# Cross-attention by quadrants of 32 queries: sums of squares as rows of 256 columns, query sums turned on VectorE, key weights rounded by ScalarE

## The chip, the cores and the metric

The kernel runs on one core of one Trainium2 chip. The metric is the device time of one execution in microseconds. Before the change it is 654.05 us, the median of 3 runs (654.0 to 654.47).

## The reference

1024 tokens of 256 features go through a gated cross-attention to a context of 1024 rows of 128 features (16 sequences of 64 tokens, each with its own 64 context rows, 16 heads of 128), and then through a gated block of causal self-attention and a mixture of experts (16 experts, 6 taken, and a shared one). All weights and tokens are float32. The change touches the cross-attention alone:

```python
x = x + tanh(g_xattn[0]) * xattn(layernorm(x), ctx_1024, Wq, Wk, Wv, Wo, gq, gk)

def xattn(hidden, ctx, Wq, Wk, Wv, Wo, gq, gk):
    q = (hidden @ Wq).reshape(B, Sq, H, D)       # B = 16, Sq = 64, H = 16, D = 128
    k = (ctx @ Wk).reshape(B, Skv, H, D)         # Skv = 64
    v = (ctx @ Wv).reshape(B, Skv, H, D)
    q = q * rsqrt(mean(q * q, -1) + 1e-5) * gq
    k = k * rsqrt(mean(k * k, -1) + 1e-5) * gk
    attn = softmax(einsum("bqhd,bkhd->bhqk", q, k) / sqrt(D))
    return einsum("bhqk,bkhd->bqhd", attn, v).reshape(B, Sq, H * D) @ Wo
```

## The kernel before

**Stages.** The tokens are handled in two halves of 512 (HT), 8 sequences each. Three kinds of stage follow each other, each for both halves: cross-attention (a), self-attention (b) and the experts' chunks (m). Stage a goes over 8 pairs of heads for each half, so over 16 pairs, and `cross_pair` holds the order of one pair, written out by hand once for each engine. Engines meet by semaphores; a pair `u` is worked on while the projections of the next one (`nxt`) run, the output of the one before (`prev`) is added, and the weights of the one after next (`after`) are split.

**Precision.** Projections and outputs are made in three matmuls of float32r with both operands split in a rounded part (`_hi`) and its rest (`_lo`). The rounded part of the query and key weights is cast by VectorE (`split_queries`, `split_keys`, L1356 and L1368) and the rest is taken by GpSimd (L1573). SyncE loads the next weights into `raw_a` once the rests are taken. Scores, sums of squares and context values are plain float32 matmuls.

**A pair on TensorE** (`cross_pair`): `norm_q` (L659), `scores` (L682), `context_values` of prev (L703), key and query projections of nxt (L525), the two outputs of prev (L552) around the second query projection, in the first half also `value_out` (L648), the turn of the attention (L690), and `norm_k` for nxt (L668). `norm_q` sums the squared queries over the 128 features: the squares of a sequence (64 columns) are the weights and a column of ones streams, so that a sum comes out as one element for each query's partition, 16 matmuls a pair, two column groups of 64. `norm_k` streams the squared keys past 64 columns of ones, 2 matmuls of 512 columns, so that each sum lies in all 64 partitions of its sequence. `scores` makes 64x64 blocks, two sequences above each other.

**The chain beside it.** VectorE adds the variance term of the tokens to the query sums (`add_variance`, L1302), ScalarE takes logarithm and root of both sums (`log_k`, `root_k`, `log_q`, `root_q`; L992, L1001, L988, L997), VectorE multiplies the scores by both roots (`scale_scores`, L1314 and L1317), takes the maximum (L1323), then the rests of prev's context values (`split_context_values`, `pv_lo`, L1290), and subtracts the maximum (L1328). ScalarE takes the exponential, VectorE normalises (L1338) and moves the next queries out of PSUM (`take_q`, L1344), with `split_queries` and `split_keys` in between. ScalarE squares queries and keys (L965, L974) and moves turned rows (`take_rows`, L1011) and context values (`take_context_values`, L1022). TensorE waits for ln_q before it projects into the same bank again, for pv_lo before it adds prev's output, for the attention before its turn, for the squares and qt before `norm_q` and `scores`.

**Pieces of token preparation** are laid beside some pairs by `plan_of` and run on VectorE and ScalarE: in the first half statistics (after pair 3, so ahead of the sums of pair 4), the norm (after pair 4) and the turn (pair 5); in the second half statistics (after pair 8 + 1), norm (after 8 + 2), mean squares on ScalarE (in 8 + 3), scale (after 8 + 4) and turn (8 + 5).

Of the kernel before, what the change touches and what calls it, by code (L numbers as in the profile page):

```python
# [32 lines left out]
P = 128  # L33
# [160 lines left out]
def flamingo_layer(nc, x, ctx_t, ctx, head_a, head_b, pair_v, chunk_m, small, out, shared_units):  # L194
# [15 lines left out]
    GROUPS = 2  # L210
    G = 2 * NT
# [18 lines left out]
    with ExitStack() as stack:  # L230
# [60 lines left out]

        gs, gu = ln_k[:].rearrange("p g k -> p (g k)"), r_k[:].rearrange("p g k -> p (g k)")
# [8 lines left out]
        eps_var, ssq = sb("eps_var", [P, HALVES, NT]), sb("ssq", [P, G])  # L301
# [42 lines left out]
        var_ready, rough = sem("var_ready"), sem("rough")  # L344
# [13 lines left out]
        def sequence_at(u, t, s):  # L358

            if u.kind == "a":  # L360
                return t * SPB + s
            return t // 2 * 4 + s * 2 + t % 2

# [4 lines left out]
        def by_row(ap, row):  # L368

            return ap.rearrange("p h (b r n) -> p h b r n", r=SPB, n=P)[:, :, :, row, :]  # L370
# [146 lines left out]
        def _(pe):  # L517
# [134 lines left out]
            def norm_q(u):  # L652

                pe.wait_ge(A["sq_q"], u.of(1))
                pe.wait_ge(A["qt"], u.of(0))
                for h in range(2):
                    for b in range(NS):
                        t, s = divmod(b, SPB)
                        last = nc.tensor.matmul(bank_q[s * SEQ:(s + 1) * SEQ, h * NT + t:h * NT + t + 1],  # L659
                                                sq_q[:, h, b * SEQ:(b + 1) * SEQ], ones[:], start=True, stop=True)  # L660
                last.then_inc(A["ssq_done"], 1)

            def norm_k(u):

                pe.wait_ge(A["sq_k"], u.of(1))
                for s in range(SPB):
                    keys = sq_k[:].rearrange("p h (t s k) -> p (h t) s k", s=SPB, k=SEQ)[:, :, s, :]
                    last = nc.tensor.matmul(bank_p[s * SEQ:(s + 1) * SEQ, :], ones_of[:], keys, start=True, stop=True)  # L668
                last.then_inc(A["ssk_done"], 1)

            def scores(u):
# [3 lines left out]
                pe.wait_ge(stage["kt"], u.of(1))  # L675
                for h in range(2):
                    for b in range(NS):
                        t, s = b // SPB, b % SPB
                        at = sequence_at(u, t, s) * SEQ
# [4 lines left out]
                last.then_inc(stage["scores"], 1)  # L684
# [76 lines left out]
            def release(held):  # L761
                for semaphore, value in held:
                    pe.wait_ge(semaphore, value)

# [129 lines left out]
        def _(act_e):  # L894
# [95 lines left out]
            def log_k(u):  # L990
                act_e.wait_ge(A["ssk_done"], u.n)
                nc.scalar.activation(ln_k[:], groups(bank_p[:]), ACT.Ln, bias=eps5[:, 0:1]).then_inc(A["ln_k"], 1)  # L992
# [6 lines left out]
            def root_k(u):  # L999
                act_e.wait_ge(A["ln_k"], u.n)  # L1000
                nc.scalar.activation(r_k[:], ln_k[:], ACT.Exp, scale=-0.5).then_inc(A["r_k"], 1)  # L1001
# [734 lines left out]
```

## Time and profile before

| | |
|---|---|
| median of 3 runs | 654.05 us |
| profiled execution | 653.9 us |
| its span (first to last instruction) | 651.8 us |
| TensorE matmul busy | 644.9 us, 99% |
| VectorE busy | 457.5 us, 70% |
| ScalarE busy | 318.4 us, 49% |
| GpSimd busy | 251.4 us, 39% |
| stage a, from the first key sums to the last turn | 13 to 204 us of the span |

The times of the engines are sums over the whole span; matmuls overlap each other in the records, so a busy TensorE is not one at its peak. In the views, PE is TensorE, DVE is VectorE, ACT is ScalarE and POOL is GpSimd. A row of the timeline is one instruction, or a run of like ones, with its start, its length and the operands by the program's names. Two records stand for each plain float32 matmul.

### The profile page before, as it was taken

What the parts mean: (1) busy time and instruction counts of PE and PEld (TensorE: products, weight loads), DVE (VectorE), ACT (ScalarE), POOL (GpSimd) and SP (SyncE); (2) the same over time, 40 slices, a digit from 0 to 9 for tenths busy, and PEclk for the clock granted to TensorE, in tenths of its full rate; (3) what the DMA queues carried; (4) which work ended last, traced back from release to release, by engine and by line L of the source; (5) the groups of instructions that cost most, each with busy time, mean ns of one, the idle gap of its engine ahead of it and who ended that gap; (6) DMA issues with size and microseconds to landing.
All of it is one profiled execution on the core that took longest, in us unless ns stands there. A gap on an engine that the chain in (4) does not pass through costs nothing.

```text
span 651.8 us, 16025 instructions
## 1 busy us (share of the span) xinstructions
PE 644.9 (99%) x6176; PEld 566.5 (87%) x6176; DVE 457.5 (70%) x891; ACT 318.4 (49%) x639; POOL 251.4 (39%) x336
## 2 busy tenths in 40 slices
PE   8999999999999999999999999999999999999997
PEld 6888888888888899999899999988888888888886
DVE  5867776787866788676777798666556987555556
ACT  6756656667663334333343433354476444444443
POOL 3221121121132344433343355425544755555553
PEclk9999999999999999999999999999999999999999
DMA  7522112001002222214222222103323233333332
GB/s 229 176 71 77 49 51 74 26 28 48 26 17 64 68 67 65 84 53 127 67 65 66 66 69 82 49 11 112 97 75 96 73 98 95 99 96 86 92 94 91
DMA packets 36013, 50.15 MB, mean 77 GB/s; under 512 B 4080, under 2 KB 23024, under 8 KB 35952
## 3 DMA queue, kind: packets, MB, share of 16 engines
q1 hardware_dynamic: 35376, 48.81, 25.2%
q8 instruction: 44, 0.72, 0.5%
q10 hardware_dynamic: 576, 0.48, 0.2%
q14 instruction: 17, 0.14, 0.1%
HBM read 48.22 MB, written 1.05 MB: 76 GB/s over the span
## 4 chain that ended last, share of the span: by engine, by line
PE 98%; DMA 1%; DVE 1%; SPq 0%; ACT 0%; issue 0%; DVEq 0%; ACTq 0%
PE acc L552 25%; PE bank_k L525 16%; PE bank_q L525 16%; PE bank_v L525 9%; PE bank_v L638 7%; PE bank_s L525 5%; PE bank_s L682 5%; PE bank_p L703 3%; PE bank_p L668 2%; PE bank_q L659 2%; PE bank_t L690 2%; PE bank_p L720 2%; PE bank_k L648 1%; DMA xt<-in_ctx_t 1%; PE bank_t L720 1%; PE bank_p L729 0%
## 5 line engine op out<-in xcount | busy, mean ns | idle before, releaser
L552 PE MATMUL acc<-wo_hi,pv_hi 128*128 128x256 f32 x328 | 93.1, 284 | 1.3 <-DVE pv_lo L1419 1.3
L552 PE MATMUL acc<-wo_lo,pv_hi 128*128 128x256 f32 x328 | 92.9, 283 | 0.0
L552 PE MATMUL acc<-wo_hi,pv_lo 128*128 128x256 f32 x328 | 92.0, 281 | 0.0
L1573 POOL TENSOR_TENSOR wq_lo<-raw_a,wq_hi 128x256 fp32r<-128x256 f32 x32 | 23.3, 731 | 133.6 <-DVE wq_hi L1356 133.6
L552 PEld LDWEIGHTS acc<-wo_hi,pv_hi 128*128 128x128 f32 x328 | 61.5, 188 | 5.2 <-issue 2.1
L552 PEld LDWEIGHTS acc<-wo_lo,pv_hi 128*128 128x128 f32 x328 | 61.6, 188 | 2.3
L1573 POOL TENSOR_TENSOR wq_lo<-raw_m,wq_hi 128x256 fp32r<-128x256 f32 x50 | 39.7, 793 | 61.7 <-DVE wq_hi L1375 60.2
L552 PEld LDWEIGHTS acc<-wo_hi,pv_lo 128*128 128x128 f32 x328 | 62.3, 190 | 0.0
L1419 DVE TENSOR_TENSOR pv_lo<-raw_a,pv_hi 128x512 fp32r<-128x512 f32 (+1 forms) x51 | 37.0, 727 | 32.5 <-ACT pv_hi L1048 32.3
L525 PE MATMUL bank_q<-xt_hi,wq_hi 128*128 128x512 f32 x144 | 59.8, 415 | 0.0
L970 ACT ACTIVATE kt<-bank_k 128x512 f32<-128x512 f32 x63 | 37.8, 600 | 43.4 <-PE bank_k L525 43.3
L1048 ACT ACTIVATE pv_hi<-raw_a 128x512 fp32r<-128x512 f32 (+1 forms) x51 | 31.7, 624 | 55.3 <-DVE raw_a L1414 52.1
L1406 DVE TENSOR_TENSOR r_k<-ln_k,unit_w 128x512 f32<-128x512 f32 x44 | 32.0, 727 | 35.7 <-ACT ln_k L1039 35.7
L525 PE MATMUL bank_q<-xt_hi,wq_lo 128*128 128x512 f32 x144 | 56.6, 393 | 0.0
L525 PE MATMUL bank_q<-xt_lo,wq_hi 128*128 128x512 f32 x144 | 56.4, 392 | 0.0
L1573 POOL TENSOR_TENSOR wk_lo<-raw_m,wk_hi 128x256 fp32r<-128x256 f32 x50 | 39.4, 788 | 33.7 <-ACT wk_hi L1118 33.5
L1573 POOL TENSOR_TENSOR wv_lo<-raw_v,wv_hi 128x512 fp32r<-128x512 f32 x16 | 20.6, 1288 | 72.6 <-DVE wv_hi L1382 72.6
L525 PE MATMUL bank_k<-xt_lo,wk_hi 128*128 128x512 f32 x114 | 44.8, 393 | 0.0
L525 PE MATMUL bank_k<-xt_hi,wk_hi 128*128 128x512 f32 x114 | 44.7, 392 | 0.0
L525 PE MATMUL bank_k<-xt_hi,wk_lo 128*128 128x512 f32 x114 | 44.6, 391 | 0.0
L1573 POOL TENSOR_TENSOR wq_lo<-raw_b,wq_hi 128x256 fp32r<-128x256 f32 x32 | 24.8, 776 | 49.2 <-DVE wq_hi L1359 49.2
L1573 POOL TENSOR_TENSOR wo_lo<-raw_m,wo_hi 128x256 fp32r<-128x256 f32 x50 | 40.2, 805 | 6.8 <-ACT wo_hi L1112 6.8
(216 smaller groups left out, 1908.2 us busy)
## 6 DMA issues: line engine op xcount, KB each, us to landing
raw_m<-in_chunk_m SPq DMA_DIRECT2D x50, 256.0 KB, 2.7
raw_a<-in_head_a SPq DMA_DIRECT2D x48, 192.0 KB, 2.9
raw_b<-in_head_b SPq DMA_DIRECT2D x32, 256.0 KB, 3.1
raw_m<-in_chunk_m SPq DMA_DIRECT2D x50, 128.0 KB, 2.0
raw_v<-in_pair_v SPq DMA_DIRECT2D x16, 256.0 KB, 2.8
raw_b<-in_head_b SPq DMA_DIRECT2D x32, 128.0 KB, 2.1
xs<-in_x SPq DMA_DIRECT2D x6, 128.0 KB, 3.5
out<-xs SPq DMA_DIRECT2D x3, 256.0 KB, 2.4
```

What stands on the lines that cost most here:

```text
L525: last = nc.tensor.matmul(bank[:], w[:, cols], m(k), start=n == 0, stop=n == 3 * chunks - 1)
L552: last = nc.tensor.matmul(acc[t // 2][:, (t % 2) * D:(t % 2 + 1) * D], w[:, tok], m, start=begins and n == 0, stop=True, skip_group_check= ...
L638: last = nc.tensor.matmul(bank_v[:, b * PAIR:(b + 1) * PAIR], m, w[:, cols], start=n == 0, stop=n == 3 * KD - 1)
L659: last = nc.tensor.matmul(bank_q[s * SEQ:(s + 1) * SEQ, h * NT + t:h * NT + t + 1], sq_q[:, h, b * SEQ:(b + 1) * SEQ], ones[:], start=True ...
L682: last = nc.tensor.matmul(bank_s[s * SEQ:(s + 1) * SEQ, g * SEQ:(g + 1) * SEQ], qt[:, h, tok], kt[:, h, tok], start=True, stop=True)
L703: last = nc.tensor.matmul(by_tile(value_bank(r)[:])[:, :, n, :], ctx_sb[rows, at:at + C], rows_t[rows, n], start=True, stop=True)
L720: last = nc.tensor.matmul(value_bank(r)[c * SEQ:(c + 1) * SEQ, cols], values[rows, n, width], turned[rows, cols], start=True, stop=True)
L970: nc.scalar.activation(kt[:, h], bank[:], ACT.Copy).then_inc(stage["kt"], 1)
L1048: nc.scalar.activation(pv_hi[:, u.parity, part], hh[:, part], ACT.Copy).then_inc(M["hh_hi"], 1)
L1406: nc.vector.tensor_tensor(gu, gs, weights, ALU.mult).then_inc(M["weighted"], 1)
L1419: nc.vector.tensor_tensor(pv_lo[:, u.parity, part], hh[:, part], pv_hi[:, u.parity, part], ALU.subtract)\
L1573: nc.gpsimd.tensor_tensor(lo, raw, hi, ALU.subtract).then_inc(signal, 1)
```

## The change

- `norm_q` and `norm_k` become alike: for each of four groups of sequences (`QUADS`), 32 columns of ones are the weights and 256 columns of squares stream, and the result goes to 32 partitions: 4 matmuls each, 256 columns wide, in place of 16 and of 2. A sum now lies in a row, once for each sequence's key or query, and repeated over the group's 32 partitions.
- The query sums are needed by partition. `add_variance` turns them on VectorE (`transpose` of 128x256, 32x32 blocks) into `sums_t` and adds the variance term to every 32nd element. The variance term is brought to the same order by 8 small matmuls against the unit matrix in the first pair of each half (`place_variance`), and copied to `eps_q` by VectorE.
- `scores` makes 32x64 blocks, half a sequence of queries against its 64 keys, in four column groups: 32 matmuls a pair in place of 16.
- `log_k` and `root_k` take 256 columns in place of 512; `scale_scores` broadcasts their result over the two parts of the queries.
- `take_rows`, `by_row`, `take_context_values` and `split_context_values` follow the new order of the sequences, the host lays out the context by it.
- `split_keys` in stage a, but for the first two pairs, goes from VectorE to ScalarE (`round_keys`), one after each of the two `square_q`.

```diff
+    GROUP = 32
+    QUADS = P // GROUP
...
+        half_wide = [a[:].rearrange("p g k -> p (g k)")[:, 0:HT // 2] for a in (ln_k, r_k)]
...
-        eps_var, ssq = sb("eps_var", [P, HALVES, NT]), sb("ssq", [P, G])
+        sums_t = sb("sums_t", [P, HT // 2])
+        eps_var, eps_q, ssq = sb("eps_var", [P, HALVES, NT]), sb("eps_q", [P, G // 2]), sb("ssq", [P, G])
...
-        def sequence_at(u, t, s):
-            if u.kind == "a":
-                return t * SPB + s
+        def sequence_at(t, s):
...
+        def quads(ap):
+            return ap.rearrange("p h (n j q) -> p h n j q", j=QUADS, q=SEQ)
...
         def by_row(ap, row):
...
-            return ap.rearrange("p h (b r n) -> p h b r n", r=SPB, n=P)[:, :, :, row, :]
+            return ap[:, :, row * HT // 2:(row + 1) * HT // 2]
...
             def norm_q(u):
...
                 pe.wait_ge(A["sq_q"], u.of(1))
...
-                for h in range(2):
-                    for b in range(NS):
-                        t, s = divmod(b, SPB)
-                        last = nc.tensor.matmul(bank_q[s * SEQ:(s + 1) * SEQ, h * NT + t:h * NT + t + 1],
-                                                sq_q[:, h, b * SEQ:(b + 1) * SEQ], ones[:], start=True, stop=True)
+                if u.first:
+                    place_variance(u)
+                for j in range(QUADS):
+                    last = nc.tensor.matmul(bank_q[j * GROUP:(j + 1) * GROUP, 0:HT // 2], ones_of[:, 0:GROUP],
+                                            quads(sq_q[:])[:, :, :, j, :], start=True, stop=True)
...
             def norm_k(u):
...
                 pe.wait_ge(A["sq_k"], u.of(1))
-                for s in range(SPB):
-                    keys = sq_k[:].rearrange("p h (t s k) -> p (h t) s k", s=SPB, k=SEQ)[:, :, s, :]
-                    last = nc.tensor.matmul(bank_p[s * SEQ:(s + 1) * SEQ, :], ones_of[:], keys, start=True, stop=True)
+                for j in range(QUADS):
+                    last = nc.tensor.matmul(bank_p[j * GROUP:(j + 1) * GROUP, 0:HT // 2], ones_of[:, 0:GROUP],
+                                            quads(sq_k[:])[:, :, :, j, :], start=True, stop=True)
...
             def scores(u):
...
+                if u.kind == "a":
+                    for g in range(G):
+                        h, part, n = g // 4, g // 2 % 2, g % 2
+                        for j in range(QUADS):
+                            at = (n * QUADS + j) * SEQ
+                            queries = slice(at + part * GROUP, at + (part + 1) * GROUP)
+                            last = nc.tensor.matmul(bank_s[j * GROUP:(j + 1) * GROUP, g * SEQ:(g + 1) * SEQ],
+                                                    qt[:, h, queries], kt[:, h, at:at + SEQ], start=True, stop=True)
+                    last.then_inc(A["scores"], 1)
+                    return
...
-                        at = sequence_at(u, t, s) * SEQ
+                        at = sequence_at(t, s) * SEQ
...
-                last.then_inc(stage["scores"], 1)
+                last.then_inc(B["scores"], 1)
...
+            def place_variance(u):
+                pe.wait_ge(eps_ready, u.half + 1)
+                variance = eps_var[:, u.half, :].rearrange("p (n t) -> p t n", n=2)
+                for j in range(QUADS):
+                    for part in range(2):
+                        row = j % 2 * SEQ + part * GROUP
+                        nc.tensor.matmul(bank_q[j * GROUP:(j + 1) * GROUP, HT // 2 + part * 2:HT // 2 + part * 2 + 2],
+                                         ident[:, row:row + GROUP], variance[:, j // 2], start=True, stop=True)
...
             def log_k(u):
...
-                nc.scalar.activation(ln_k[:], groups(bank_p[:]), ACT.Ln, bias=eps5[:, 0:1]).then_inc(A["ln_k"], 1)
+                nc.scalar.activation(half_wide[0], bank_p[:, 0:HT // 2], ACT.Ln, bias=eps5[:, 0:1]).then_inc(A["ln_k"], 1)
...
             def root_k(u):
...
-                nc.scalar.activation(r_k[:], ln_k[:], ACT.Exp, scale=-0.5).then_inc(A["r_k"], 1)
+                nc.scalar.activation(half_wide[1], half_wide[0], ACT.Exp, scale=-0.5).then_inc(A["r_k"], 1)
...
             def take_rows(u):
...
-                nc.scalar.activation(rows_t[:].rearrange("p n h q -> p h n q"), by_tile(bank_t[:]), ACT.Copy)\
+                nc.scalar.activation(rows_t[:].rearrange("p n h (a q) -> p (h a) n q", q=GROUP),
+                                     bank_t[:].rearrange("p (b n q) -> p b n q", n=QUADS, q=GROUP), ACT.Copy)\
...
             def take_turned(u):
...
-                    nc.scalar.activation(by_row(pv_hi[:], r), value_bank(r)[:].rearrange("p (h b n) -> p h b n", h=2, n=P),
+                    nc.scalar.activation(by_row(pv_hi[:], r), value_bank(r)[:].rearrange("p (h n) -> p h n", h=2),
...
+            def round_keys(u, h, user):
+                act_e.wait_ge(A["k_done"], user.of(h))
+                act_e.wait_ge(ld_a1[h], 16 * u.n)
+                nc.scalar.activation(wk_hi[h][:, 0:P], raw_a1[h][:, AK:AK + P], ACT.Copy).then_inc(A["wk_hi"], 1)
...
             def cross_pair(u):
...
+                after = nxt.next()
...
+                    if after.kind == "a":
+                        round_keys(after, 0, nxt)
...
+                    if after.kind == "a":
+                        round_keys(after, 1, nxt)
...
                     if kind == "x":
-                        link(nc.vector.tensor_scalar(eps_var[:, half, :], mv[:, :, 1], 1e-5, 1e-5, ALU.add, ALU.mult))
+                        nc.vector.tensor_scalar(eps_var[:, half, :], mv[:, :, 1], 1e-5, 1e-5, ALU.add, ALU.mult)\
+                            .then_inc(eps_ready, 1)
...
             def split_context_values(u):
...
-                    nc.vector.tensor_tensor(by_row(pv_lo[:], r), value_bank(r)[:].rearrange("p (h b n) -> p h b n", h=2, n=P),
+                    nc.vector.tensor_tensor(by_row(pv_lo[:], r), value_bank(r)[:].rearrange("p (h n) -> p h n", h=2),
...
             def add_variance(u):
...
-                found = bank_q[:, 0:G].rearrange("p (h t) -> p h t", h=2)
-                nc.vector.tensor_tensor(ssq[:].rearrange("p (h t) -> p h t", h=2), found,
-                                        eps_var[:, u.half, :].unsqueeze(1).to_broadcast([P, 2, NT]), ALU.add)\
+                if u.first:
+                    dve.mark(nc.vector.tensor_copy(eps_q[:], bank_q[:, HT // 2:HT // 2 + G // 2]))
+                link(nc.vector.transpose(sums_t[:], bank_q[:, 0:HT // 2]))
+                found = sums_t[:].rearrange("p (h n a q) -> p h a n q", h=2, n=2, q=GROUP)[:, :, :, :, 0]
+                variance = eps_q[:].rearrange("p (a n) -> p a n", a=2).unsqueeze(1).to_broadcast([P, 2, 2, 2])
+                nc.vector.tensor_tensor(ssq[:].rearrange("p (h a n) -> p h a n", h=2, a=2), found, variance, ALU.add)\
...
             def scale_scores(u):
...
-                    nc.vector.tensor_tensor(sc_sub[:], found, r_k[:], ALU.mult).then_inc(A["raw"], 1)
+                    by_key = half_wide[1].rearrange("p (h n) -> p h n", h=2).unsqueeze(2).to_broadcast([P, 2, 2, P])
+                    nc.vector.tensor_tensor(sc_sub[:].rearrange("p (h a n) k -> p h a (n k)", h=2, a=2),
+                                            bank_s[:].rearrange("p (h a n) -> p h a n", h=2, a=2), by_key, ALU.mult)\
+                        .then_inc(A["raw"], 1)
...
-                split_keys(after, 0, nxt)
+                if after.kind == "b":
+                    split_keys(after, 0, nxt)
...
-                split_keys(after, 1, nxt)
+                if after.kind == "b":
+                    split_keys(after, 1, nxt)
...
-    ctx_pairs = ctx.reshape(HALVES, -1, 2, P // SEQ, SEQ, C).transpose(2, 4, 0, 1, 3, 5).reshape(P, -1)
+    ctx_pairs = ctx.reshape(HALVES, 2, -1, SEQ, C).transpose(1, 3, 0, 2, 4).reshape(P, -1)
```

## Rows read from the trace of the kernel before

**Rows 1.** The page: busy times, granted clock by slices, the chain by engine.
```profile
PE 644.9 (99%) x6176; PEld 566.5 (87%) x6176; DVE 457.5 (70%) x891; ACT 318.4 (49%) x639; POOL 251.4 (39%) x336
...
PEclk9999999999999999999999999999999999999999
...
PE 98%; DMA 1%; DVE 1%; SPq 0%; ACT 0%; issue 0%; DVEq 0%; ACTq 0%
```

**Rows 2.** Timeline of PE, pair 8: start, length, engine, line, operands, count.
```profile
110.31 1.08 PE L668 MATMUL bank_p<-sq_k,ones_of 128*64 128x512 f32 x4
111.22 1.05 PE L659 MATMUL bank_q<-ones,sq_q 128*64 128x1 f32 x32
112.12 1.13 PE L682 MATMUL bank_s<-kt,qt 128*64 128x64 f32 x32
113.18 0.37 PE L703 MATMUL bank_p<-rows_t,ctx_sb 64*128 64x128 f32 x1
...
115.08 0.39 PE L525 MATMUL bank_q<-xt_hi,wq_hi 128*128 128x512 f32 x1
```

**Rows 3.** Groups by line and form, PE: count, busy us, mean ns, idle before.
```profile
L682 PE MATMUL bank_s<-kt,qt 128*64 128x64 f32 x1024 | 36.5, 224 | 0.0
...
L668 PE MATMUL bank_p<-sq_k,ones_of 128*64 128x512 f32 x64 | 17.3, 618 | 0.0
```

**Rows 4.** Timeline of PE in stage b, first and last of 64 records of L720.
```profile
336.47 0.27 PE L720 MATMUL bank_p<-rows_t,vs 64*64 64x64 f32 x1
...
336.49 0.27 PE L720 MATMUL bank_t<-rows_t,vs 64*64 64x64 f32 x1
...
337.41 0.22 PE L720 MATMUL bank_t<-rows_t,vs 64*64 64x64 f32 x1
```

**Rows 5.** Timelines of DVE, ACT and PE, pair 8, sums to output.
```profile
112.31 0.17 DVE L1302 TENSOR_TENSOR ssq<-bank_q,eps_var 128x8 f32<-128x8 f32 x1 [1.01 <-PE bank_q L659]
113.37 0.69 DVE L1314 TENSOR_TENSOR sc_sub<-bank_s,r_k 128x512 f32<-128x512 f32 x1 [0.89 <-PE bank_s L682]
...
116.09 0.68 DVE L1290 TENSOR_TENSOR pv_lo<-bank_t,pv_hi 128x512 fp32r<-128x512 f32 x1
...
112.92 0.21 ACT L997 ACTIVATE r_q<-ln_q 128x8 f32<-128x8 f32 x1
...
117.15 0.28 PE L552 MATMUL acc<-vo_hi,pv_hi 128*128 128x256 f32 x1
```

**Rows 6.** Groups by line and form, DVE and ACT: nearest to the new operations.
```profile
L1419 DVE TENSOR_TENSOR pv_lo<-raw_a,pv_hi 128x256 fp32r<-128x256 f32 x2 | 0.8, 422 | 0.2 <-ACT pv_hi L1048 0.2
...
L1142 ACT ACTIVATE wk_hi<-raw_a 128x128 fp32r<-128x128 f32 x2 | 0.6, 302 | 1.6 <-DMA raw_a<-in_head_a 1.6
```

**Rows 7.** Timeline of ACT, pair 8: squares of head 1's queries.
```profile
120.17 0.60 ACT L965 ACTIVATE sq_q<-bank_v 128x512 f32<-128x512 f32 x1 [0.70 <-PE bank_v L525]
```

**Rows 8.** Timeline of DVE, pairs 4, 11 and 13, ahead of the scaled scores.
```profile
62.41 0.17 DVE L1302 TENSOR_TENSOR ssq<-bank_q,eps_var 128x8 f32<-128x8 f32 x1
62.52 0.69 DVE L1314 TENSOR_TENSOR sc_sub<-bank_s,r_k 128x512 f32<-128x512 f32 x1
...
148.38 0.68 DVE L1314 TENSOR_TENSOR sc_sub<-bank_s,r_k 128x512 f32<-128x512 f32 x1
...
168.31 0.47 DVE L1368 CAST wk_hi<-raw_a 128x128 fp32r<-128x128 f32 x1
...
171.61 0.69 DVE L1314 TENSOR_TENSOR sc_sub<-bank_s,r_k 128x512 f32<-128x512 f32 x1
```

**Rows 9.** Timelines of ACT and PE, ahead of pair 12.
```profile
156.36 0.60 ACT L965 ACTIVATE sq_q<-bank_v 128x512 f32<-128x512 f32 x1
...
157.69 1.05 PE L659 MATMUL bank_q<-ones,sq_q 128*64 128x1 f32 x32
```

**Rows 10.** Timelines of DVE and PE, pair 1.
```profile
22.65 0.68 DVE L1344 TENSOR_TENSOR qt<-bank_v,gqk 128x512 f32<-128x512 f32 x1
...
23.68 1.13 PE L682 MATMUL bank_s<-kt,qt 128*64 128x64 f32 x32
```

More of the change, by code:

```diff
@@ L343, in flamingo_layer @@
         cw_ready = sem("cw_ready")
-        var_ready, rough = sem("var_ready"), sem("rough")
+        var_ready, eps_ready, rough = sem("var_ready"), sem("eps_ready"), sem("rough")
         y_ready = sem("y_ready")
```

## The prediction

> **What bounds the kernel now.** I read the page first: TensorE is busy 99% of the span and holds 98% of the chain that ended last, and its granted clock is full in every slice [rows 1]. So an edit is worth what it takes from or adds to TensorE, unless it makes TensorE wait. Then the timeline of TensorE over one pair of heads of cross-attention (stage a has 16 pairs; I number them 0 to 15, the rows show pair 8). Three small blocks stand between the turn of the attention and the context values: the key sums 0.91 us (110.31 to 111.22), the query sums 0.90 (to 112.12), the scores 1.06 (to 113.18) [rows 2]. The grouped view has their counts [rows 3]: 4 records a pair for the key sums, two for each fp32 matmul, and 32 for the scores (half of the 1024 are stage b's); rows 2 have 32 for the query sums. The change touches just these three. Last I read VectorE and ScalarE beside them, since the same edit puts work there, and looked in each pair at how far ahead of TensorE they are.
>
> **Part 1, sums of the key squares (L668).** Now: two column groups of 64 stream 512 columns each, in two passes. One record is 618 ns long and the four take 0.91 us, so both groups stream at once. After: four groups of 32 with 256 columns each. If all four stream at once the block halves to 0.455; I add 0.025 for a start that doesn't shrink (an estimate): 0.48, saved 0.43.
>
> **Part 2, sums of the query squares (L659).** Now the squares are the weights: 32 records with one column streamed, 0.028 from one to the next, 0.90 us. After, the ones are the weights and 256 columns stream in four groups, as in part 1 but without a change of tiling ahead: 0.45. Saved 0.45.
>
> **Part 3, scores (L682).** 32 records of 64 queries become 64 of 32, in four groups instead of two; each group still streams 16 records of 64 columns. Now the first and the last start lie 1.13 - 0.22 = 0.91 apart [rows 2, 3], 16 rounds of 0.06. The nearest block with four tiles at once is L720 in stage b: the first four records start within 0.02 us, and all 64 between 336.47 and 337.41 [rows 4]: 0.94, again 0.06 a round. I take 0.03 more than now.
>
> TensorE's sum for a pair: 0.43 + 0.45 - 0.03 = 0.85. The unknown is the width: L720 shows four tiles at once, but as two row halves by two column halves; no row has four column groups over all 128 rows. Bounds: four wide without any loss, 0.95 a pair; or two wide as now, where parts 1 and 2 save nothing (twice 256 columns is 512) and part 3 costs 16 more rounds of 0.06. I take four wide, because two column groups show no loss against one and L720 shows that 64 loads and matmuls can be issued in 0.94. The Trainium skill gives, in "TensorE: Matmul & The Clock Gate", section "Measured speedup vs the span model", 2.38 times for three column tiles; carried on to four at the same loss that is an estimate of 3.2 at a time, close to the first case of rival A, and no run here shows it.
>
> **Part 4, variance placed by TensorE (first pair of each half).** 8 matmuls, 16 records, four rounds of 0.06: 0.24, twice. In pair 0 it lies in a wait, in pair 8 it is paid. VectorE adds one small copy from PSUM there (0.17, as ssq).
>
> **Part 5, query sums turned on VectorE.** add_variance was one operation of 0.17 [rows 5]. It gets a 128x256 transpose from PSUM ahead, with a wait on its own result. No row is a transpose; the nearest is fp32 arithmetic on 128x256, 0.42 [rows 6]. I take 0.42 + 0.04 = 0.46, bounds 0.3 and 0.95 (twice, and a gap). In a plain pair it is hidden: ssq starts at 112.31, and sc_sub stands idle 0.89 until the scores are there (113.37). r_q is ready at 113.13 and not needed before sc_sub ends at 114.06; TensorE asks for ln_q, which is earlier still, before the queries' projection at 115.08 [rows 2, 5]. All of it comes 0.46 later and in time. That cover goes only if the turn takes over 1.3 us.
>
> **Part 6, key weights rounded by ScalarE.** VectorE loses two casts a pair. The first lets qt of head 1 start 0.14 earlier, the second frees 0.39 where GpSimd works beside it (0.47 long at 168.31 [rows 8]), 0.2 elsewhere. ScalarE gains two of 128x128, 0.30 each [rows 6] and about 0.2 where they follow straight on, and loses half the columns of two 512-wide activations (ln_k, r_k): about even. The first cast stands ahead of sq_q of head 1, which waits 0.70 for TensorE in a plain pair [rows 7]: hidden, and the price where that cover is gone is 0.2. Behind it GpSimd (wk_lo) and SyncE's reload of raw_a wait; what they make is used in the next pair, some 10 us on. If the load of two pairs ahead isn't there in pair 0, ScalarE stands instead of VectorE, some tenths once. The other access patterns (rows of 32 in rows_t, unbroken rows of pv_hi and pv_lo, broadcast keys in sc_sub) move the same element counts: nothing, bounds plus or minus 0.05 an operation, under the same cover.
>
> **What comes late next.** With TensorE 0.88 sooner at the end of the scores, the other engines have that much less cover. The tightest link in every pair is pv_lo: its second part ends 116.77, the output that reads it starts 117.15 [rows 5]; about 0.3 can go. It hangs on sc_sub, so a late sc_sub stalls TensorE by its lateness less 0.3. In plain pairs sc_sub still starts on the scores' end. Where VectorE has a piece of token preparation it doesn't [rows 8]:
> - Pair 4: statistics right up to sc_sub at 62.52, which is just the scores' end. The casts give nothing back here (what follows them waits for ScalarE). New: 62.52 + 0.46, where TensorE would allow 61.64. Late 1.34, stall 1.0.
> - Pair 11: 148.38 - 0.54 (casts) + 0.46 = 148.30; allowed, by the scores' end, 147.34. Late 0.96, stall 0.65.
> - Pair 13: 171.61 - 0.53 + 0.46 = 171.54; allowed 170.73. Late 0.8, stall 0.5.
> - Pairs 5 and 10, in the same way: 0.1 each.
> - Pair 12: mean squares on ScalarE hold sq_q of head 1 to 156.96, the query sums start 157.69 [rows 9]. They could start 0.43 and the scores 0.88 sooner, and the cast puts 0.2 ahead of sq_q and so of qt: stall 0.4.
> Together 2.75 given back.
> The first two pairs aren't bound by TensorE's work: in pair 1 the scores (23.68) start 0.35 after qt is ready (22.65 + 0.68) [rows 10]. Pair 0 gains nothing, pair 1 some 0.2 by the cast that goes.
>
> **Sum.** 14 pairs x 0.85 = 11.9; + 0.2 (pair 1); - 0.24 (pair 8); - 2.75: 9.1. The profiled run took 653.9 with a span of 651.8, so 2.1 lie around the span and the run is 0.15 below the median. Span 642.7, and 654.05 - 9.1 = 645.0.
>
> **Rivals.**
> - A, less width or a binding VectorE, still faster. If four column groups do three groups' work at a time, each sum costs 0.57 to 0.6 and a round of scores 0.08: 0.31 + 0.33 - 0.32 = 0.32 a pair, 14 pairs 4.5, nearly nothing given back: 649.5. If the turn takes 0.95, pairs 4, 5, 10, 11 and 13 lose 0.5 more each: 647.5; were every pair late by 0.3, 650. Against it: the hole of 0.89 in rows 5.
> - B, issue binds. A floor on the time between record starts would hit the scores, whose count doubles: at the 0.028 of L659 [rows 2] the 64 take 1.8 against 0.94, which eats the 0.88: 654, no change. Rows 4 speak against it: 64 records in 0.94, 0.015 each. The Trainium skill states such a floor, 25 ns from start to start for small matmuls ("TensorE: Matmul & The Clock Gate", section "Wait — 56ns, not 53.3ns?"), which would make it 651; the trace of L720 disagrees with it, for different tiles, and the measurement decides.
> - C, slower: only two column groups work at once. Place: L682, in all 16 pairs; 16 more rounds of 0.06 are +0.95 each, and parts 1 and 2 save nothing: 654 + 15 = 669. It decides once a round of four costs over 0.06 + 0.88/16 = 0.115, that is, under 2.1 tiles at a time. Against it: all tiles that rows 2 and 4 open run together.
> - D, better: the full 0.95 and no stalls: 14 x 0.95 = 13.3, 640.8.
>
> **How the numbers follow.** Forecast 0.66 (641 to 648.5), A 0.17 (to 652), B 0.03, C 0.10, D 0.02, the change does nothing 0.02. The range for 8 in 10 runs from 641.0, just above D, to 651.5, into A; C is left out. 0.2% is 1.3 us, about what can be told from no change. Faster 0.85, within 0.05, slower 0.10.
>
> **What the profile would show.** Right: key sums 0.48 and query sums 0.45 a pair, their four groups starting within 0.03; scores 1.0 to 1.1; pairs without a piece 0.85 closer together; short stalls of the output in pairs 4, 11 and 13, ended by pv_lo; a turn of 0.4. Wrong: third and fourth group starting as the first two end (C); scores of 1.8 (B); sc_sub late in plain pairs (A). What would break it first is the width.

## The result, and the profile after the change

The changed kernel takes 644.08 us, the median of 4 runs (643.71 to 644.27), against 654.02 (653.64 to 654.47) for the one before: a ratio of 0.9844 (95% interval 0.9832 to 0.9857), 9.9 us. The profiled execution has a span of 641.8 us, 10.0 under that of before. The forecast was 645.0, with 641.0 to 651.5 around it.

The page of the changed kernel, the same parts as [rows 1] (busy us, share, number of instructions; granted clock in 40 slices; the chain that ended last):

```profile
PE 633.0 (99%) x6400; PEld 553.5 (86%) x6400; DVE 460.7 (72%) x881; ACT 318.0 (50%) x667; POOL 252.6 (39%) x336
...
PEclk9999999999999999999999999999999999999999
...
PE 91%; DVE 6%; ACT 1%; issue 1%; DMA 1%; SPq 0%; DVEq 0%; ACTq 0%
```

TensorE lost 11.9 us of busy time while the span lost 10.0. The clock is full as before. VectorE, which held 1% of the chain, now holds 6%: some of the gain was given back there.

TensorE's timeline of two pairs, first pair 8, the one of [rows 2], then pair 3, a plain one (start, length, engine, line, operands, count; L673 are the key sums, L788 the placed variance, L665 the query sums, L688 the scores, L719 the context values):

```profile
105.30 0.64 PE L673 MATMUL bank_p<-sq_k,ones_of 128*32 128x256 f32 x8
105.75 0.29 PE L788 MATMUL bank_q<-eps_var,sm 128*32 128x2 f32 x14
105.88 0.38 PE L665 MATMUL bank_q<-sq_q,ones_of 128*32 128x256 f32 x1
...
106.31 1.11 PE L688 MATMUL bank_s<-kt,qt 128*32 128x64 f32 x64
107.36 0.37 PE L719 MATMUL bank_p<-rows_t,ctx_sb 64*128 64x128 f32 x1
```

```profile
45.59 0.64 PE L673 MATMUL bank_p<-sq_k,ones_of 128*32 128x256 f32 x8
46.05 0.61 PE L665 MATMUL bank_q<-sq_q,ones_of 128*32 128x256 f32 x8
46.48 1.08 PE L688 MATMUL bank_s<-kt,qt 128*32 128x64 f32 x64
47.48 0.37 PE L719 MATMUL bank_p<-rows_t,ctx_sb 64*128 64x128 f32 x1
```

Read the starts: the key sums hold TensorE 0.46 us (before 0.91), the query sums 0.43 (0.90), the scores 1.00 (1.06). Eight records of one block fit into 0.64 us, though one alone is 391 ns long by the groups: four column groups stream at once. The groups by form, as in [rows 3], with the new operations of VectorE and ScalarE behind them (count, busy us, mean ns, idle before):

```profile
L688 PE MATMUL bank_s<-kt,qt 128*32 128x64 f32 x1024 | 17.3, 219 | 0.1
...
L673 PE MATMUL bank_p<-sq_k,ones_of 128*32 128x256 f32 x128 | 10.2, 391 | 0.0
...
L1060 ACT ACTIVATE wk_hi<-raw_a 128x128 fp32r<-128x128 f32 x28 | 8.5, 305 | 0.0
...
L1341 DVE STREAM_TRANSPOSE sums_t<-bank_q 128x256 f32<-128x256 f32 x16 | 7.1, 445 | 2.1 <-PE bank_q L665 1.5
```

From one block of query sums to the next, a plain pair of the first half takes 11.51 us where it took 12.49, and one of the second half 10.66 where it took 11.62: 0.97 saved. Five pairs are longer than that by a stall: pair 4 by 1.08, pair 5 by 0.19, pair 10 by 0.07, pair 11 by 1.13, pair 13 by 1.19; pair 12 by 0.1 at most. That makes 3.8 us, each against the spacing of before less 0.97 (pair 12 against a plain 10.66: its own spacing was 11.77 before, 0.15 over the plain one, so against that it lost nothing). The waits of TensorE on VectorE's pv_lo name them (us in total, times, longest); before, the same line (then L1290) held TensorE 0.6 us in two waits:

```profile
PEld acc L558 <- DVE pv_lo L1328: 3.7, 6, 0.8
...
PE acc L558 <- DVE pv_lo L1328: 1.4, 4, 0.4
```

VectorE ahead of that wait, in pair 4 and in pair 11 (before: [rows 8]):

```profile
57.40 0.69 DVE L1438 TENSOR_TENSOR vo_lo<-bank_k,vo_hi 128x512 fp32r<-128x512 f32 x1 [1.19 <-ACT vo_hi L1064]
58.01 1.40 DVE L1246 BATCH_NORM_STATS2 bn<-xs 128x6 f32<-128x256 f32 x4
...
59.93 0.45 DVE L1341 STREAM_TRANSPOSE sums_t<-bank_q 128x256 f32<-128x256 f32 x1
60.41 0.17 DVE L1344 TENSOR_TENSOR ssq<-sums_t,eps_q 128x8 f32<-128x8 f32 x1
60.50 0.69 DVE L1356 TENSOR_TENSOR sc_sub<-bank_s,r_k 128x512 f32<-128x512 f32 x1
```

```profile
134.90 0.69 DVE L1382 TENSOR_TENSOR attn<-ex,ex_inv 128x512 f32<-128x512 f32 x1
...
136.93 0.44 DVE L1400 CAST wq_hi<-raw_a 128x256 fp32r<-128x256 f32 x1
137.29 0.41 DVE L1226 TENSOR_TENSOR st<-st 128x4 f32<-128x4 f32 x1
137.73 0.66 DVE L1227 TENSOR_TENSOR st<-st 128x4 f32<-128x4 f32 x1
138.42 0.39 DVE L1228 TENSOR_SCALAR st<-st 128x4 f32<-128x4 f32 x1
...
140.35 0.44 DVE L1341 STREAM_TRANSPOSE sums_t<-bank_q 128x256 f32<-128x256 f32 x1
```

In pair 4 the statistics of the token preparation (L1246) stand ahead of the turn; sc_sub starts at 60.50 where the scores' last record started at 58.85, 1.65 later instead of the plain 0.36. In pair 11 it is 1.71, in pair 13 1.73. The rows of pair 11 hold a second thing: three operations on 4 columns take 0.41, 0.66 and 0.39 us. Before the change the first operation behind the casts was as stretched, and the cast ahead of it too (pair 11, before):

```profile
145.06 0.47 DVE L1368 CAST wk_hi<-raw_a 128x128 fp32r<-128x128 f32 x1
145.46 0.70 DVE L1189 TENSOR_TENSOR st<-st 128x4 f32<-128x4 f32 x1
```

### The profile page after: what moved, and what is told of

Its sections match the earlier page's. It is cut to its first block, busy times and chain, and to the rows that moved or that the text cites. A ratio compares the mean times of both kernels' runs of the same rounds, so it can differ in the third digit from the quotient of the medians.

```text
span 641.8 us, 16518 instructions
## 1 busy us (share of the span) xinstructions
PE 633.0 (99%) x6400; PEld 553.5 (86%) x6400; DVE 460.7 (72%) x881; ACT 318.0 (50%) x667; POOL 252.6 (39%) x336
## 4 chain that ended last, share of the span: by engine, by line
PE 91%; DVE 6%; ACT 1%; issue 1%; DMA 1%; SPq 0%; DVEq 0%; ACTq 0%
PE acc L558 25%; PE bank_q L531 15%; PE bank_k L531 15%; PE bank_v L531 8%; PE bank_v L644 7%; PE bank_s L531 5%; PE bank_s L698 3%; PE bank_p L736 2%; PE bank_p L719 2%; PE bank_t L706 2%; PE bank_s L688 2%; PE bank_p L673 1%; PE bank_k L654 1%; PE bank_q L665 1%; DVE pv_lo L1328 1%
```

## The experiments

All runs stood beside runs of the kernel before (medians 653.7 to 653.8); the changed kernel's 644.08 is the mark for each.

### The width: scores group after group

```diff
-for g in range(G):
-    h, part, n = g // 4, g // 2 % 2, g % 2
-    for j in range(QUADS):
+for j in range(QUADS):
+    for g in range(G):
+        h, part, n = g // 4, g // 2 % 2, g % 2
```

> The changed kernel with the 64 score records of a pair in another order: all 16 of one column group, then the next group, instead of one of each in turn. Same work, same results. Theory W (the gain is width: four column groups stream at once, and only neighbours in issue order can overlap): each record then stands alone at 0.056 us, the block grows from 0.90 to about 3.6 us, +2.7 in each of 16 pairs, while the stalls of the late pairs go: some 684 us. Rival I (the block is bound by issue, 128 loads and matmuls at 0.007 each, and not by the groups): order doesn't matter, 644.

Measured: 672.85 us (672.62 to 673.07), ratio 1.0291 (1.0271 to 1.0312). TensorE in a plain pair, and the group of the scores (compare 17.3 us busy and a mean of 219 above: the records are as long as before, but cover each other no more):

```profile
51.45 0.61 PE L665 MATMUL bank_q<-sq_q,ones_of 128*32 128x256 f32 x8
51.88 3.16 PE L688 MATMUL bank_s<-kt,qt 128*32 128x64 f32 x64
54.97 0.37 PE L719 MATMUL bank_p<-rows_t,ctx_sb 64*128 64x128 f32 x1
```

```profile
L688 PE MATMUL bank_s<-kt,qt 128*32 128x64 f32 x1024 | 50.6, 220 | 0.1
```

The same 64 records in the other order take 3.09 us instead of 1.00: only records of different column groups run together. So the width is real. Issue is no bound for the changed order either: a record of one group starts 0.056 us behind the one before it in both orders. The expected 684 was too high: at 0.056 apart 64 records would make 3.6 us, but in the single records a second row of starts begins at 52.56, while the first group's go on to 52.72, so that the groups overlap at their borders.

### Query sums back to columns

The key sums stay rows in four groups, and the turn on VectorE goes.

```diff
-for j in range(QUADS):
-    last = nc.tensor.matmul(bank_q[j * GROUP:(j + 1) * GROUP, 0:HT // 2], ones_of[:, 0:GROUP], quads(sq_q[:])[:, :, :, j, :], ...)
+for g in range(G):
+    ...
+    for j in range(QUADS):
+        at = (n * QUADS + j) * SEQ + part * GROUP
+        last = nc.tensor.matmul(bank_q[j * GROUP:(j + 1) * GROUP, g:g + 1], sq_q[:, h, at:at + GROUP], ones[:], ...)
...
-link(nc.vector.transpose(sums_t[:], bank_q[:, 0:HT // 2]))
```

> The changed kernel with the query sums as before the change in kind: squares as weights, one column of ones streamed, but in four groups of 32 (64 records a pair), no turn on VectorE. Keys, scores and ScalarE's casts stay changed. Theory W: what the rows of 256 columns save on TensorE is real, and a round of four tiny records costs 8 instructions of 0.007 = 0.056, so 0.90 against 0.43: +0.47 in 14 pairs is +6.6, less some 2.4 that the late pairs get back without the turn: 648.3 us. Rival L (a block of tiny records is bound by its loads, and 32 columns load in half the time of 64): about 0.45 to 0.5, no dearer than the rows, and the turn is saved: 641.5 to 642.

Measured: 651.6 us (649.01 to 652.13), ratio 0.9959 (0.9946 to 0.9972). Both theories missed it. TensorE in a plain pair, and then where it stops, in pairs 1, 12 and 14:

```profile
52.13 0.74 PE L668 MATMUL bank_q<-ones,sq_q 128*32 128x1 f32 x64
52.75 1.10 PE L691 MATMUL bank_s<-kt,qt 128*32 128x64 f32 x64
```

```profile
23.19 0.98 PE L691 MATMUL bank_s<-kt,qt 128*32 128x64 f32 x54
27.09 0.64 PE L691 MATMUL bank_s<-kt,qt 128*32 128x64 f32 x10 [2.92 <-issue]
...
160.63 0.47 PE L531 MATMUL bank_q<-xt_hi,wq_hi 128*128 128x512 f32 x1 [0.68 <-issue]
...
182.27 0.32 PE L691 MATMUL bank_s<-kt,qt 128*32 128x64 f32 x7 [0.41 <-issue]
```

As columns in four groups the query sums take 0.62 us, against 0.43 as rows: 0.2 a pair, 2.8 over 14 pairs, less the 2.3 that the missing turn gives back in pairs 4, 5, 10, 11 and 13. So columns gain from the four groups too (0.90 to 0.62), which lies between the two theories: cheaper than W's 0.90, dearer than L's 0.45 to 0.5. The rest comes from something that neither had. In the midst of pair 1's scores TensorE stands 2.92 us, waiting for nothing that the profile shows, and comes back at a lower clock: pair 1 takes 17.93 us instead of 12.39. Two shorter stops of the same kind follow in pairs 12 and 14, 0.68 and 0.41 us.

### The same, with the early transfers issued later

```diff
 reload_a1(2)
-load_v(b0)
-for h in range(2):
-    load_b1(b0, h); load_b2(b0, h); load_m1(...); load_m2(...)
 for n in range(1, HALVES * PAIRS):
     ...
         reload_a1(n + 2)
+    if n == 2:
+        load_v(b0)
+        for h in range(2):
+            load_b1(b0, h); load_b2(b0, h); load_m1(...); load_m2(...)
```

> The kernel with query sums as columns (651.6 us, 7.5 over the changed one, of which 2.92 us are one stop of TensorE within the second pair's scores, with a granted clock of about one half after it) with one more edit: the first transfers of the second and third stage (values, weights of the self-attention and of the feed-forward) are issued only after the third pair's loads instead of behind the second reload. Theory F: the stop comes from those transfers, which fill the DMA queues when TensorE wants its next instructions; then the stop is gone and the clock stays full: 647 (646 to 648), the rest of the loss being the narrower query sums. Rival: the stop has nothing to do with the transfers, 651 to 652, with a gap of the same kind in the trace.

Measured: 650.4 us (649.5 to 651.23). The stop is still there, at the same record (and so are the two shorter ones, 0.52 and 0.66 us), so theory F falls. TensorE, and two stretches of the engine table (busy us of PE, PEld, DVE, ACT and POOL with counts, granted clock, DMA share, GB/s):

```profile
22.91 0.98 PE L692 MATMUL bank_s<-kt,qt 128*32 128x64 f32 x54
26.54 0.35 PE L692 MATMUL bank_s<-kt,qt 128*32 128x64 f32 x9 [2.65 <-issue]
```

```profile
27.50:30.90 3.40, 3.40 (x16) 2.60 (x15) 3.26 (x6) 2.10 (x4) 0.00 (x0) 0.53 0.01 2
34.00:37.00 3.00, 3.00 (x21) 2.71 (x20) 2.93 (x7) 1.72 (x5) 0.72 (x2) 1.00 0.01 3
```

After standing for 2.65 us, TensorE is granted half its clock (0.53: the level of 1.2 GHz) for some 3.4 us. Pair 1 takes 16.31 us instead of 12.39: 2.65 of that is the stop, 0.2 the wider sums, and about 1.1 is left for the clock. In the run above this one it stood 2.92, and its granted clock was 0.50 from 27 to 33 us and 1.00 again from 34 on. The traces show what TensorE stands for. Behind the 54th record, between 24.0 and 25.2, the queue that carries instructions brings 16 KB:

```profile
q8 instruction: 1, 0.02, 4.8%
```

Over the span this queue made 53 such transfers, against 46 in the changed kernel, which has 896 matmuls and as many loads fewer: 256 instructions of TensorE for each transfer. So it is TensorE's program that arrives there. Two more readings say that TensorE waits for it. Each of the six stops of the two runs ends 1.3 to 1.5 us after such a transfer has ended (25.80 to 27.09, 159.24 to 160.63 and 180.88 to 182.27 in the run above; 25.06 to 26.54, 157.15 to 158.59 and 179.04 to 180.44 here). And counted over TensorE's own instructions in the trace (matmuls, loads and its sequencer's), the stops lie 4609 and 766 instructions apart in both runs, which is 18 and 3 times 256 within two. In the changed kernel a transfer of the same queue falls between 25 and 26, and TensorE doesn't stop. Why the transfer comes late in the one and in time in the other was not tried, and stays open.

### The turn, made twice

```diff
-link(nc.vector.transpose(sums_t[:], bank_q[:, 0:HT // 2]))
+for _ in range(2):
+    link(nc.vector.transpose(sums_t[:], bank_q[:, 0:HT // 2]))
```

> The changed kernel with the turn of the query sums done twice (0.45 + 0.03 us more on VectorE in every pair). Theory V (the turn is hidden in plain pairs by the hole of 0.31 us ahead of the scaled scores and 0.3 us ahead of the output, and on the path in the late ones): +0.48 in pairs 1, 4, 5, 10, 11 and 13, 2.4 to 2.9 in all: 646.7 us. Rival P (the turn lies on the path of every pair): +0.48 x 16 = 7.7, 651.8. Rival N (it is hidden everywhere): 644.1.

Measured: 646.89 us (646.77 to 647.17), ratio 0.9894 (0.9877 to 0.991), +2.8. Plain pairs stay 11.51 and about 10.7 apart; pair 1 grows by 0.88, pair 4 by 0.49, 5 by 0.48, 10 by 0.39, 11 by 0.36, 13 by 0.48. So the turn is free in plain pairs and on the path wherever VectorE is late: at 0.36 to 0.49 for its 0.48 in five pairs, and at 0.88 in pair 1. The hole that hides it, in pair 3, first the changed kernel, then this one:

```profile
47.69 0.69 DVE L1356 TENSOR_TENSOR sc_sub<-bank_s,r_k 128x512 f32<-128x512 f32 x1 [0.31 <-PE bank_s L688]
```

```profile
47.95 0.93 DVE L1342 STREAM_TRANSPOSE sums_t<-bank_q 128x256 f32<-128x256 f32 x2
...
49.01 0.68 DVE L1357 TENSOR_TENSOR sc_sub<-bank_s,r_k 128x512 f32<-128x512 f32 x1
```

With the second turn the hole is gone and sc_sub starts 0.09 late; the slack of pv_lo before the output, 0.35, takes that up.

### The key weights' rounding, alone and undone

The kernel before with this part of the change alone:

> The kernel before with one part of the change alone: the rounding of the key weights on ScalarE. The sums of squares stay columns. There TensorE is bound by its own records in all pairs, and no late pair has a stall that a shorter VectorE queue could take away, so the theory (sums carry the gain) says 653.8 (653.5 to 654.2), as before. The rival that the casts carry a share of the 9.9 us: 652 or less.

Measured: 653.63 us (653.24 to 654.8, 11 runs), ratio 0.9999 (0.999 to 1.0008). Nothing, as the theory had it.

The changed kernel with this part undone:

```diff
 split_queries(after, 0, nxt)
-if after.kind == "b":
-    split_keys(after, 0, nxt)
+split_keys(after, 0, nxt)
```

(the same for head 1, and the two calls of round_keys leave ScalarE).

> The changed kernel with the rounding of the key weights back on VectorE in all pairs (ScalarE loses two casts a pair). The prediction took .54 us of VectorE out of each late pair by this move (.27 a cast), so with it undone pairs 4, 11 and 13 should stall .54 us more and pairs 5 and 10 about as much: +1.6 to +2.5 us, 645.7 to 646.6. The two traces gave only .17 to .20 us between the weights' product and the next squares of pairs 11 and 13, although two casts had gone: by that reading (M, mis-sized term) it is 3 times .2 = +.6 us, 644.7 (644.3 to 645.0). If the key casts carried a part of the gain in plain pairs too (C), more than 3 us are lost, and the spacing of plain pairs grows over 11.51 and 10.66.

Measured: 645.39 us (644.65 to 645.65), +1.3, ratio 0.9868 (0.9853 to 0.9883). Outside pair 1 the sum is M's, not the prediction's, though not its shares: pair 4 and pair 5 grow by nothing (0.01, 0.03), pair 10 by 0.39, pair 11 by 0.06, pair 13 by 0.20, and pair 12 shrinks by 0.10, together 0.6. On VectorE itself, from the attention's product to the turn, the two casts are worth 0.19 in pair 11 (5.64 instead of 5.45), 0.19 in pair 13 (5.59 instead of 5.40) and 0.40 in pair 10 (4.70 instead of 4.30). The rest is pair 1, which neither had: 13.27 instead of 12.39, from 22.69 to 35.96. Pair 4 shows why its casts were worth nothing there:

```profile
58.82 0.69 DVE L1434 TENSOR_TENSOR vo_lo<-bank_k,vo_hi 128x512 fp32r<-128x512 f32 x1 [0.79 <-ACT vo_hi L1064]
```

VectorE waits for ScalarE's vo_hi behind the casts, 0.79 us with them and 1.19 without: they only shorten a wait.

### GpSimd's work beside VectorE cut away

```diff
+cols = D if u.n < 3 else 8
-rest(wq_lo[h][:], raw_a1[h][:, AQ:AQ + D], wq_hi[h][:], A["wq_lo"])
+rest(wq_lo[h][:, 0:cols], raw_a1[h][:, AQ:AQ + cols], wq_hi[h][:, 0:cols], A["wq_lo"])
```

(wk_lo in the same way.)

> The changed kernel with GpSimd's subtractions that take the rests of the query and key weights in the first stage cut to 8 columns from the third pair on, so that GpSimd is nearly idle beside VectorE there (most of those rests are left as they were, so the output differs). Two casts left VectorE in each late pair, but only .2 of their .54 us came free, while the operations around them got longer. Contention theory (G): those operations stretch because GpSimd works beside them; then the query weights' cast (.44 us in those pairs) falls back to .3, and pairs 11 and 13 give back about .3 to .5 us each: 643.2 (642.8 to 643.6). The rival that the lateness is VectorE's own queue, whatever GpSimd does: 644.1 (643.9 to 644.3).

Measured: 641.43 us (641.15 to 641.5), ratio 0.9811 (0.9796 to 0.9826), 2.65 under the changed kernel, beyond what the contention theory had asked. VectorE in pair 11, the same rows as above:

```profile
134.67 0.69 DVE L1382 TENSOR_TENSOR attn<-ex,ex_inv 128x512 f32<-128x512 f32 x1
...
136.68 0.28 DVE L1400 CAST wq_hi<-raw_a 128x256 fp32r<-128x256 f32 x1
136.88 0.15 DVE L1226 TENSOR_TENSOR st<-st 128x4 f32<-128x4 f32 x1
137.07 0.19 DVE L1227 TENSOR_TENSOR st<-st 128x4 f32<-128x4 f32 x1
137.29 0.17 DVE L1228 TENSOR_SCALAR st<-st 128x4 f32<-128x4 f32 x1
...
138.99 0.44 DVE L1341 STREAM_TRANSPOSE sums_t<-bank_q 128x256 f32<-128x256 f32 x1
```

The cast takes 0.28 instead of 0.44, the three small operations 0.15, 0.19 and 0.17 instead of 0.41, 0.66 and 0.39. From the attention's product to the turn it is 4.32 us instead of 5.45. Pair 11 is 1.04 shorter, pair 13 1.12, pair 1 0.26; pairs 4 and 5, whose late piece (statistics) lies behind the rests of GpSimd and not beside them, stay as they were.

### The piece of token preparation in the hole

In the changed kernel VectorE has a hole of 1.1 us in each pair while ScalarE takes the exponentials. The second piece of the preparation moves there:

```diff
 subtract_max(u)
+prepare_piece(*piece_at(u, 1), u)
 ...
     split_value_out(u)
-prepare_piece(*piece_at(u, 1), u)
```

(and ScalarE makes its rough root one piece earlier, since it is wanted sooner).

> The changed kernel with the pieces of token preparation that stand at the end of a pair of stage a on VectorE moved into the hole of the same pair in which VectorE waits for the exponentials; ScalarE's rough root one pair earlier. Theory V (3.7 us of the gain are given back because VectorE reaches the sums and scores late in pairs 4, 5, 10, 11 and 13): the pieces of 2 to 2.3 us fill a hole of 1.1 and the 1.25 to 2.1 us by which the attention is early, the stalls ahead of the outputs of these pairs go: 640.5 us. Rival H (VectorE has no room left, the lateness only moves to the attention's turn): 1 to 1.5 us less, 642.8 or more.

Measured: 640.3 us (640.06 to 640.65), ratio 0.9795 (0.9778 to 0.9811): faster than both kernels. VectorE in pair 4:

```profile
51.58 1.40 DVE L1246 BATCH_NORM_STATS2 bn<-xs 128x6 f32<-128x256 f32 x4
...
58.21 0.45 DVE L1341 STREAM_TRANSPOSE sums_t<-bank_q 128x256 f32<-128x256 f32 x1
58.69 0.17 DVE L1344 TENSOR_TENSOR ssq<-sums_t,eps_q 128x8 f32<-128x8 f32 x1
59.17 0.69 DVE L1356 TENSOR_TENSOR sc_sub<-bank_s,r_k 128x512 f32<-128x512 f32 x1 [0.31 <-PE bank_s L688]
```

The statistics stand 6.6 us before the turn, the hole ahead of sc_sub is back at 0.31, and the pairs 4, 10 and 11 take 11.51, 10.65 and 10.65. Only pair 12 stalls a little longer (10.95 instead of 10.75).

With the second turn added to this version:

> The version with the pieces of token preparation moved into VectorE's wait for the exponentials (640.3 us, no late pairs left among 4, 5, 10, 11 and 13), with a second turn of the query sums behind the first, as a price of .48 us per pair on VectorE. In the changed kernel the same second turn cost 2.8 us: nothing in plain pairs, .88 in pair 1 and .4 to .5 in each of pairs 4, 5, 10, 11 and 13. If those losses come only from the place of the pieces (theory L), here just pair 1 pays, and pair 12 perhaps .2: 641.3 (641.0 to 641.7). The rival that the turn itself is on the path wherever the pieces stand (T): 643.1.

Measured: 641.15 us (640.97 to 641.55), +0.85, and all of it is pair 1 (13.27 instead of 12.39). So, but for pair 1, the turn was on the path through the place of the pieces alone.

With the early transfers issued later:

> The version with the pieces of token preparation moved into VectorE's wait for the exponentials (640.3 us), with one more edit: the first transfers of the second and third stage (values, weights) are issued behind the third pair's loads instead of behind the second reload, which leaves the DMA queues free from 10 to 25 us. Pairs 0 and 1 take longer than a plain one. If the loads of the first stage's own weights are held up by those transfers (S), pair 1 gets its weights sooner: 639.5 or less. The rival that pairs 0 and 1 wait for VectorE and ScalarE alone (N): 640.3 (640.0 to 640.6).

Measured: 640.38 us (640.14 to 640.64): the same. The share of the DMA engines between 10 and 25 us fell from 0.82 to 0.44, and the first pairs did not get shorter (8.30 and 12.41 us from query sums to query sums; 8.43 and 12.39 without this edit). So these transfers do not bound pair 1. In the changed kernel TensorE's weight loads wait for VectorE three times between 21 and 29 us: 0.57 us for the attention, 0.55 for qt and 0.77 for pv_lo.

## Why the prediction was right, and where it was off

The forecast's mechanism held: 645.0 against 644.08. Its steps:

- **Parts 1 and 2, the sums.** 0.48 and 0.45 forecast, 0.46 and 0.43 measured. The choice of four wide without loss, over the 2.38 times for three column tiles that the Trainium skill gives ("TensorE: Matmul & The Clock Gate", section "Measured speedup vs the span model"), was borne out: four groups halve a block that two groups with twice the columns had filled, with nothing left over.
- **Part 3, the scores.** Mis-sized in sign: +0.03 forecast, -0.06 measured. Sixteen rounds of 0.056 replace sixteen of 0.06. With the 0.04 more that parts 1 and 2 saved, the gain per pair is 0.97, not 0.85: 0.12 in each that the forecast left out. The floor of 25 ns from start to start that the Trainium skill states ("TensorE: Matmul & The Clock Gate", section "Wait — 56ns, not 53.3ns?") does not hold here: the first and the last of 64 records start 1.08 - 0.22 = 0.86 us apart, 14 ns each, and rival B falls with it.
- **Part 4, the variance.** 0.24 forecast for pair 8, 0.13 measured (105.75 to 105.88).
- **Part 5, the turn.** 0.46 forecast, 0.45 measured and 0.48 to the next operation. Hidden in plain pairs, as said. The cover was oversized: it was put at 1.3 us, from the chain of r_q and ln_q, and is 0.8; the turn's 0.45 lay within both. The first thing to come late is sc_sub itself, after the turn's 0.45 plus the 0.31 of the hole; the run with two turns, 0.93, had it 0.09 late.
- **Part 6, the casts: the term that was mis-sized.** 0.54 us less on VectorE in the late pairs of the second half was forecast. From the attention's product to the squares' operation behind the sums, pair 11 went from 5.62 to 5.45 us and pair 13 from 5.59 to 5.40 (before, up to ssq; after, up to the turn, which stands in its place): 0.2. The kernel before with the casts moved shows the same two steps (5.42 and 5.38), and so does the changed kernel with them undone. The 0.39 of the second cast had been read as its own price, but it was mostly the price of running beside GpSimd (0.22 long where GpSimd is not at work, 0.47 beside it): when the cast goes, the operations behind it move into that stretch (before 0.70 and 0.38 us for 4 columns, then 0.17; now 0.41, 0.66 and 0.39). The cut of GpSimd's work showed it, with 1.1 us given back in a pair. "Nothing given back in pair 4" was right, and undoing the casts confirmed it.
- **What comes late next.** The pairs were named rightly, the link (pv_lo before the output) too. The sizes: pair 4 1.08 (forecast 1.0), 5 and 10 0.19 and 0.07 (0.1 each), 11 1.13 (0.65), 13 1.19 (0.5), 12 0.1 (0.4). Together 3.8 against 2.75; pairs 11 and 13 carry the whole miss. The casts that freed 0.2 instead of 0.54, and ends that came 0.12 earlier on TensorE in each pair and so took more of the cover, make 0.46 a pair: all of pair 11's miss of 0.48, and two thirds of pair 13's 0.69; the rest there is not explained. Pair 12's stall was probably hidden by pair 11's, which gives ScalarE time: in the version without the latter, pair 12 stalls 0.3, near the 0.4 forecast.
- **The first pairs.** Nothing in pair 0 and 0.2 in pair 1 were forecast. The query sums of pair 2 start 0.86 earlier (34.53 after 35.39): 0.12 before pair 0's sums (no more than the start moves from one profiled execution to another: 13.64 to 14.32 in the runs whose stage a has sums as rows), 0.46 from there to pair 1's, 0.28 to pair 2's. The 0.46 of pair 0 belongs to the sums and scores, since it is there with the casts undone (8.37 us) and not with the casts alone (8.76, as before): pair 0 was forecast to gain nothing. In pair 1 VectorE decides: with the casts undone or the turn made twice it takes 13.27, longer than the 12.66 of before. The one row read ahead of its scores [rows 10] wasn't the whole chain.

The sum of the measured terms: 13 intervals of 0.97 from pair 2 on are 12.6, the first pairs 0.86, the placed variance -0.1, the stalls -3.6 (pair 12 lost nothing against before): 9.8, and pair 15's query sums start 9.78 earlier (193.56 before, 183.78 after). Another 0.2 comes behind them, which makes the 10.0 of the span. The forecast's 9.1 was short by 0.9 in the blocks (11.9 for 12.8, although it counted a whole pair more), by 0.7 in the first pairs and by 0.1 in the variance, and had 0.9 too little in the stalls. The errors partly cancelled, which was luck: the number was nearer than its parts.

Rival A is out by the sums' 0.46 and 0.43 (it asked for 0.57 to 0.6) and by the hole of 0.31 in plain pairs, C by the same blocks (it asked for no saving there and 0.95 more in the scores) and by the experiment that takes the width of the scores away and loses 2.09 us a pair by it. D's 640.8, every stall gone, is what the version with the piece in the hole reached: 640.3.

## What to carry to other kernels

When a short block on the bottleneck engine is cut, list for each repetition how late the other engines' next result comes, and where a piece of side work stands ahead of it; moving that piece into a wait of the same engine may be worth as much as pricing the change well (here 3.8 us, beside the change's own 9.9). Price an operation that goes away by what follows it in the same stretch, not by its own length: if it was stretched by a neighbour engine, its successors inherit the stretching. And before more instructions are put on an engine, count them: the runs with 14% more of them stopped three times for their own program, once for 2.65 to 2.92 us, and ran at half the clock for some us after that.

## What the runs showed of the hardware that was not expected

- Four column groups of 32 work at once over all 128 rows: 64 fp32 records of 64 columns in 1.00 us in turn, and in 3.09 us group after group.
- Operations of VectorE on 4 columns take 0.15 to 0.19 us alone and 0.38 to 0.70 beside GpSimd's subtractions of 128x256 and 128x128; a cast of 128x256 takes 0.28 alone and 0.44 beside them.
- A turn of 128x256 fp32 in blocks of 32 on VectorE, from PSUM, takes 0.445 us.
- In both kernels that had 7296 matmuls instead of 6400 TensorE stopped three times for its instructions, 2.65 to 2.92 us once and 0.41 to 0.68 us twice. Each stop ended 1.3 to 1.5 us after a 16 KB transfer of the instruction queue had ended. After the long one it was granted 1.2 GHz for some 3.4 us in the one and 6 to 7 us in the other.
